# Second attention: both halves of a pair's values in one piece in the odd slot, a chunk in every even slot, and another order on ScalarE

## The chip, the cores and the metric

The kernel runs on one core of one Trainium2 chip. The metric is the device time of one launch in microseconds (us), the median of three runs. TensorE does the matmuls and transposes and writes PSUM; VectorE (DVE), ScalarE (ACT) and GpSimd (POOL) work beside it. Each engine runs its own list of instructions in order, and they meet at semaphores: `pe.wait_ge(ev("x"), k)` holds TensorE until counter x has reached k, and `.then_inc(ev("x"), 1)` raises it when the instruction ends.

## The reference, cut to what matters

Two blocks, each a layer norm with modulation, an attention and a feed-forward part. The change lies in the second block's attention, over x of shape 2 x 1024 x 128:

```python
H, Dk = 16, 64
q, k, v = shape(x @ Wq), shape(x @ Wk), shape(x @ Wv)      # b h s d
scores = einsum('bhqd,bhkd->bhqk', q, k)
weights = softmax(scores + position_bias, axis=-1)
context = einsum('bhqk,bhkd->bhqd', weights, v)
return context.transpose(0, 2, 1, 3).reshape(B, S, H * Dk) @ Wo
```

## The kernel before, in words

Two heads of one batch make a unit; there are 8 pairs of heads and 2 batches, so `UNITS = 16`. A unit has `TB = 8` tiles of 128 queries, `TILES = 128` in all. A tile n has two heads (hd 0 and 1) and goes through these steps:

- **Scores** (`pe_scores`, L407): 12 matmuls into `SC[0]` and `SC[1]`, one for each head. They wait for `nmax_done` of the tile before, since VectorE must have read `SC`.
- **Biased maximum** (`dve_biased`, L566): VectorE adds the position strip, writes `soft` and the maximum, once per head.
- **Exponential** (`act_exp`, L527): ScalarE, once per head, `ACTIVATE` and then `ACTIVATION_READ_ACCUMULATOR`, whose end is `exp_done`.
- **Turn** (`pe_turn`, L427): 16 transposes of one head into the two PT banks. Both heads use the same banks. So the second head's turn waits for `ptA_out`, ScalarE's copy of the first head's (`act_turned`, L512, 128x1024), and the next tile's first turn waits for the second head's two copies: VectorE's half (`dve_turned`, L574, `ptB_out`) and ScalarE's half (`act_turned_half`, L519, `ptB_half`).
- **Values** (`pe_values`, L444): two tiles (2g and 2g+1) make a group g, "pair" in the title; their turned weights lie in `PTs[:, g % 2]`. The values take 8 key blocks for 256 queries. They are done in two halves of 4 key blocks (16 matmul instructions each), half 0 in an even slot and half 1 in the next, odd one. ScalarE copies the result out (`act_ctx`, L536), at the end of the odd slot.
- **Output weights** (`pe_wo`, L463): in the next even slot, into the right half of `CX` and the left of `MI`, scaled by VectorE (`dve_wo`, L583) and added by POOL (`pool_add`, L607, L610).

Beside them go the **chunks**: the projections for the next unit, six for each, four of q and k (`pe_chunk`, L388) and two of v (L386), all in bank `MI`. ScalarE copies a chunk out (`act_chunk`, L330 or L321, `high_out`), POOL splits q and k into two parts (`pool_chunk`, L354 and L356, `low_out`). `pe_wo` writes `MI` too and so waits for the `high_out` of the chunk in its own slot.

The order is written out by hand in slots. Slot n holds, on TensorE: scores of tile n+1; turn of tile n, first head; a chunk if there is one; half the values of a group; turn of tile n, second head; in even slots the output weights. On ScalarE: the copy of the first turn; the exponential of tile n+1, first head; the chunk's copy; the exponential, second head; the half copy of the second turn; in odd slots `act_ctx`. From the third unit on the chunks lie in the slots `chunk_slots` of a unit, for the first two units in `second_slots` and `third_slots`, which fill every slot from 4 to 15. The last unit has no chunks after it.

Of the kernel before, what the change touches and what calls it, by code (L numbers as in the profile page):

```python
# [25 lines left out]
TB = S // P  # L26
# [18 lines left out]
TILES = UNITS * TB  # L45
GROUPS = TILES // 2
# [19 lines left out]
def build(nc, rel_hot, L0_attn_x, L0_attn_Wq, L0_attn_bq, L0_attn_Wk, L0_attn_bk, L0_attn_Wv, L0_attn_bv,  # L66
# [4 lines left out]
    with ExitStack() as ctx:  # L71
# [127 lines left out]
        def ev(name):  # L199

            if name not in sems:
                sems[name] = ctx.enter_context(nc.semaphore("s_" + name))
            return sems[name]
# [58 lines left out]

        chunks = [("q", 0), ("k", 0), ("q", 1), ("k", 1), ("v", 0), ("v", 1)]
        first_chunks = [("q", 0), ("k", 1), ("v", 1), ("k", 0), ("q", 1), ("v", 0)]
        chunk_slots = (0, 1, 2, 3, 5, 7)
        second_chunks = [("q", 0), ("k", 1), ("k", 0), ("q", 1), ("v", 0), ("v", 1)]
        second_slots, third_slots = (4, 5, 6, 7, 8, 9), (2, 3, 4, 5, 6, 7)

# [4 lines left out]
        def chunk_of(u, c):  # L273

            return (first_chunks, second_chunks, chunks)[min(u, 2)][c]
# [5 lines left out]
        def middle(n):  # L281

            u, i = n // TB, n % TB
            if n in chunk_at:
                return ("chunk",) + chunk_at[n]
            if u == UNITS - 1 and i in turn_slots:
                return "turn", turn_slots.index(i), 0
            return "none", 0, 0

        def chunks_until(n):  # L290

            return 6 + sum(1 for i in chunk_at if i <= n)

        def turns_until(n):

            return sum(1 for i in turn_slots if (UNITS - 1) * TB + i <= n)
# [13 lines left out]
        def chunk_bank(u, c):  # L310

            return four[c % 4] if u == 0 else MI[:, :]

        def act_chunk(act, u, c):

            kind, q = chunk_of(u, c)
            act.wait_ge(ev("proj_full"), 2 * (6 * u + c + 1))
            if kind == "v":
                if u >= 2:
                    act.wait_ge(ev("pv_done"), 4 * (u - 1))  # L320
                act.copy(V1[:, u % 2, 4 * q:4 * q + 4, :].rearrange("p t d -> p (t d)"), chunk_bank(u, c)).then_inc(ev("high_out"), 1)  # L321
                return
            sign = -1.0 if kind == "q" else 1.0
            if u == 0:
                act.mul(qk[0][:, 0 if kind == "q" else 2, q * CK:(q + 1) * CK], chunk_bank(u, c), sign).then_inc(ev("high_out"), 1)
                return

            if 4 * u + c >= 6:
                act.wait_ge(ev("low_out"), 4 * u + c - 1)
            act.mul(raw_qk[:, c % 2, :], chunk_bank(u, c), sign).then_inc(ev("high_out"), 1)  # L330
# [61 lines left out]
        def pe_scores(pe, n):  # L392

            u, i = n // TB, n % TB
            if n == 0:
                pe.wait_ge(ev("low_out"), 3)
            elif n == TB // 2 or i == 0 or (u == 1 and i == TB // 2):
                pe.wait_ge(ev("low_out"), 4 * u + (3 if (u, i) == (1, 0) else 4))
            if n == 0:
                pe.wait_ge(ev("hT_ready"), 10)  # L400
            else:
                pe.wait_ge(ev("nmax_done"), 2 * n)
            for k in range(2):
                for m, (qp, kp) in enumerate(((0, 2), (0, 3), (1, 2))):
                    for hd in range(2):
                        mine = slice(hd * DK, hd * DK + DK)
                        ins = pe.matmul(SC[hd][:, k * CK:(k + 1) * CK], qk[u % 2][mine, qp, i * P:(i + 1) * P],  # L407
                                        qk[u % 2][mine, kp, k * CK:(k + 1) * CK], start=(m == 0), stop=(m == 2))
                        if k == 1 and m == 2:
                            ins.then_inc(ev("scores"), 1)  # L410
# [21 lines left out]
        def pe_values(pe, g, half):  # L432

            if half == 0:
                pe.wait_ge(ev("ptA_out"), 2 * g + 2)
                pe.wait_ge(ev("ptB_out"), 2 * g + 2)
                pe.wait_ge(ev("ptB_half"), 2 * g + 2)
                pe.wait_ge(ev("ctx_out"), g)
            else:
                pe.wait_ge(ev("woA_out"), g)  # L440
            vb = g // 4 % 2
            for t in range(4 * half, 4 * half + 4):
                for hd in range(2):
                    ins = pe.matmul(CX[hd * DK:(hd + 1) * DK, 0:2 * P], V1[:, vb, t, hd * DK:(hd + 1) * DK],  # L444
                                    PTs[:, g % 2, hd, t, :], start=(t == 0), stop=(t == TB - 1))
                    if half == 1 and t == TB - 1:
                        ins.then_inc(ev("pv_done"), 1)

        def pe_wo(pe, g):

            u = g // 4
            n = 2 * g + 4
            pe.wait_ge(ev("ctx_out"), g + 1)
            if g >= 1:
                pe.wait_ge(ev("woB_out"), g)
            pe.wait_ge(ev("high_out"), chunks_until(n))
            if turns_until(n):
                pe.wait_ge(ev("wT_ready"), turns_until(n))
            for t in range(2):
                for hd in range(2):  # L460
                    mine = slice(hd * DK, hd * DK + DK)
                    dst = CX[:, (2 + t) * P:(3 + t) * P] if hd == 0 else MI[:, t * P:(t + 1) * P]
                    ins = pe.matmul(dst, ctxs[mine, g % 4, t * P:(t + 1) * P], wog[mine, u % B, u // B, :],  # L463
                                    start=(hd == 1 or (g == GROUPS - 1 and t == 0)), stop=True, skip_group_check=True)
                    if t == 1:
                        ins.then_inc(ev("woA_full" if hd == 0 else "woB_full"), 1)

        def pe_weights(pe, j):

            n = (UNITS - 1) * TB + turn_slots[j]  # L470
            if j == 0:
                pe.wait_ge(ev("ld_ffn"), 16 * 9)
                pe.wait_ge(ev("high_out"), 6 * UNITS)
            else:
                pe.wait_ge(ev("wT_ready"), j)
            pe.wait_ge(ev("woB_out"), (n - 5) // 2 + 1)
            for w in range(4 * j, min(4 * j + 4, 13)):
                ins = pe.transpose(MI[:, (w % 4) * P:(w % 4 + 1) * P], raw[:, w, :], ident[:, :])
            ins.then_inc(ev("ffn_turned"), 1)

        def pe_slot(pe, n):
            if n + 1 < TILES:
                pe_scores(pe, n + 1)
            if 0 <= n < TILES:
                pe_turn(pe, n, 0)
            what, a, c = middle(n)
            if what == "chunk":
                pe_chunk(pe, a, c)
            elif what == "turn":
                pe_weights(pe, a)  # L490
            if 2 <= n < TILES + 2:
                pe_values(pe, (n - 2) // 2, n % 2)
            if 0 <= n < TILES:
                pe_turn(pe, n, 1)
            if n >= 4 and n % 2 == 0:
                pe_wo(pe, (n - 4) // 2)

        def turned_in(hd):

            return PTW[:, :].rearrange("p (r t q) -> p r t q", r=2, t=TB)  # L500
# [6 lines left out]
        def act_turned(act, n):  # L507

            act.wait_ge(ev("ptA_full"), 2 * n + 2)
            if n >= 4:  # L510
                act.wait_ge(ev("pv_done"), n // 2 - 1)
            act.copy(turned_out(n, 0), turned_in(0)).then_inc(ev("ptA_out"), 1)  # L512

        def act_turned_half(act, n):

            act.wait_ge(ev("ptB_full"), 2 * n + 2)
            if n >= 4:
                act.wait_ge(ev("pv_done"), n // 2 - 1)
            act.copy(turned_out(n, 1)[:, 1, :, :], PT[1][:, :].rearrange("p (t q) -> p t q", t=TB)).then_inc(ev("ptB_half"), 1)  # L519
# [18 lines left out]
        def act_slot(act, n):  # L538
            if 0 <= n < TILES:
                act_turned(act, n)  # L540
            if n + 1 < TILES:
                act_exp(act, n + 1, 0)
            what, a, c = middle(n)
            if what == "chunk":
                act_chunk(act, a, c)
            elif what == "turn":
                act.wait_ge(ev("ffn_turned"), a + 1)
                w = min(4, 13 - 4 * a)
                act.copy(wT[:, 4 * a:4 * a + w, :].rearrange("p w d -> p (w d)"), MI[:, 0:w * P]).then_inc(ev("wT_ready"), 1)
            if n + 1 < TILES:  # L550
                act_exp(act, n + 1, 1)
            if 0 <= n < TILES:
                act_turned_half(act, n)
            if n >= 3 and n % 2 == 1:
                act_ctx(act, (n - 3) // 2)
# [1283 lines left out]
```

## Time and profile before

| | us |
|---|---|
| median of 3 runs (lowest to highest) | 948.13 (948.01 to 949.83) |
| the profiled execution, its own time | 956.01 |
| its span, first to last instruction | 954.3 |
| TensorE busy in the span | 902.3 (95%) |
| ScalarE busy | 642.4 (67%) |
| VectorE busy | 588.0 (62%) |
| GpSimd busy | 306.5 (32%) |

The trace is of one execution, whose own time is 0.8% over the median; rows are in its time. A busy share is an average over the span; TensorE's ends are modelled, so that its matmuls overlap in the rows. A start is given as us from the start of the span.

### The profile page before, as it was taken

To read this page: it belongs to the slowest core of one execution; us is meant where nothing else is said; L and a number is where in the kernel's file an instruction comes from. 1 tells how busy PE (TensorE), PEld (TensorE's weight loads), DVE (VectorE), ACT (ScalarE), POOL (GpSimd) and SP (SyncE) were. 2 spreads that over 40 slices of the span, in tenths; PEclk is the share of its full clock that TensorE was granted. 3 is DMA by queue.
4 is the path that set the end of the run, shared out by engine and by line. 5 is a ranking of instruction groups with operands and counts; after the bars stand their busy time and mean duration, and the time that the engine had idled before them with its cause. 6 is when DMAs were issued, how large, how long until landed. Compare 5 with 4: busy or idle time off the path is not lost. (4 is left out here: it accounts for less than half of the span.)

```text
span 954.3 us, 25417 instructions
## 1 busy us (share of the span) xinstructions
PE 902.3 (95%) x10209; PEld 665.0 (70%) x10209; DVE 588.0 (62%) x1348; ACT 642.4 (67%) x1094; POOL 306.5 (32%) x393
## 2 busy tenths in 40 slices
PE   8997994599999999999999999999999999998898
PEld 5685773376777776767777776767677776776677
DVE  6556112675666666666666666666666666676895
ACT  3551341487788777878787878887878778874244
POOL 5133803524423233241423333242322324115310
PEclk9998898799999999999999999999999999999899
DMA  8400621000020001002000200200020010000001
GB/s 240 155 2 23 213 88 53 26 1 2 2 92 2 3 25 70 2 2 93 1 3 1 93 2 2 92 2 2 2 92 2 2 33 10 3 1 2 1 12 34
DMA packets 27128, 35.48 MB, mean 37 GB/s; under 512 B 6042, under 2 KB 21716, under 8 KB 26836
## 3 DMA queue, kind: packets, MB, share of 16 engines
q1 hardware_dynamic: 25988, 31.76, 10.2%
q0 software_dynamic: 1024, 2.10, 0.7%
q8 instruction: 82, 1.34, 0.6%
q14 instruction: 34, 0.28, 0.1%
HBM read 28.48 MB, written 5.37 MB: 35 GB/s over the span
## 5 line engine op out<-in xcount | busy, mean ns | idle before, releaser
L566 DVE CUSTOM_DVE_ANT_0 soft<-SC,strips 128x1024 f32<-128x1024 f32 x256 | 303.3, 1222 | 78.3 <-PE SC L407 77.4
L527 ACT ACTIVATE soft<-soft,nmax 128x1024 f32<-128x1024 f32 x256 | 294.2, 1150 | 6.5 <-DVE nmax L566 6.5
L444 PE MATMUL CX<-PTs,V 128*64 128x256 f32 x2048 | 245.1, 381 | 0.0
L512 ACT COPY PTs<-PT 128x1024 f32<-128x1024 f32 x128 | 129.6, 1012 | 135.7 <-PE PT L427 135.7
L407 PE MATMUL SC<-qk 64*128 64x512 f32 x1536 | 210.8, 406 | 3.3 <-DVE nmax L566 1.8
L427 PEld LDWEIGHTS PT<-ident,soft 64*128 64x128 f32 x4096 | 159.6, 140 | 72.0 <-issue 32.5
L444 PEld LDWEIGHTS CX<-PTs,V 128*64 128x64 f32 x2048 | 143.0, 137 | 93.0 <-issue 35.5
L574 DVE COPY PTs<-PT 128x512 f32<-128x512 f32 x128 | 88.5, 692 | 164.5 <-PE PT L427 164.5
L427 PE MATMUL PT<-ident,soft 64*128 64x64 f32 x4096 | 177.1, 226 | 5.7 <-ACT soft L527 3.0
L407 PEld LDWEIGHTS SC<-qk 64*128 64x128 f32 x1536 | 136.7, 187 | 27.2 <-issue 2.1
L607 POOL TENSOR_TENSOR x<-x,wo_out 128x256 f32<-128x256 f32 x64 | 47.1, 736 | 209.3 <-DVE wo_out L583 209.3
L354 POOL CAST qk<-raw_qk 128x512 fp32r<-128x512 f32 x60 | 36.7, 612 | 237.0 <-ACT raw_qk L330 237.0
L356 POOL TENSOR_TENSOR qk<-raw_qk,qk 128x512 fp32r<-128x512 f32 x60 | 77.6, 1294 | 4.8
L519 ACT COPY PTs<-PT 128x512 f32<-128x512 f32 x128 | 74.0, 578 | 0.8 <-PE PT L427 0.7
L388 PE MATMUL MI<-hT,wpair 128*64 128x512 f32 x244 | 65.8, 617 | 0.9 <-ACT hT L863 0.9
L527 ACT ACTIVATION_READ_ACCUMULATOR soft<-soft,nmax 128x1 f32 x256 | 49.3, 193 | 0.0
L610 POOL TENSOR_TENSOR x<-x,wo_out 128x256 f32<-128x256 f32 x64 | 47.1, 735 | 5.0
L463 PE MATMUL CX<-wog,ctxs 64*128 64x128 f32 x256 | 42.4, 286 | 0.1
L463 PE MATMUL MI<-wog,ctxs 64*128 64x128 f32 x256 | 42.4, 286 | 0.0
L1005 ACT ACTIVATE probsT<-SC,cols 128x512 f32<-128x512 f32 x32 | 21.9, 689 | 26.7 <-PE SC L1757 26.6
L947 ACT ACTIVATE probsT<-SC,cols 128x384 f32<-128x384 f32 x32 | 18.6, 580 | 28.1 <-PE SC L1662 26.5
L330 ACT ACTIVATE raw_qk<-MI 128x512 f32<-128x512 f32 x60 | 35.2, 586 | 0.3 <-PE MI L388 0.3
(280 smaller groups left out, 999.8 us busy)
## 6 DMA issues: line engine op xcount, KB each, us to landing
strips<-bias_vec SPq DMA_DIRECT2D x8, 1920.0 KB, 8.3
arena<-in_L_ffn_w SPq DMA_DIRECT2D x1, 2048.0 KB, 12.4
slots_in<-arena SPq DMA_DIRECT2D x1, 1536.0 KB, 8.6
arena<-slots_in SPq DMA_DIRECT2D x8, 192.0 KB, 3.7
slots_out<-arena SPq DMA_DIRECT2D x8, 192.0 KB, 2.0
x<-in_L_attn_x SPq DMA_DIRECT2D x2, 512.0 KB, 4.3
out<-x SPq DMA_DIRECT2D x4, 256.0 KB, 2.3
arena<-in_L_wmod SPq DMA_DIRECT2D x2, 384.0 KB, 5.4
```

What stands on the lines that cost most here:

```text
L356: pool.tensor_tensor(qk[u % 2][:, k + 1, at], raw_qk[:, c % 2, :], qk[u % 2][:, k, at].bitcast(F32), ALU.subtract).then_inc(ev("low_out"), 1)
L388: ins = pe.matmul(bank[mine, :], wpair[:, p % 2, "qk".index(kind), mine], rhs, start=True, stop=True)
L407: ins = pe.matmul(SC[hd][:, k * CK:(k + 1) * CK], qk[u % 2][mine, qp, i * P:(i + 1) * P], qk[u % 2][mine, kp, k * CK:(k + 1) * CK], start= ...
L427: ins = pe.transpose(PT[r][:, t * DK:(t + 1) * DK], soft[mine, n % RING, hd, t * P:(t + 1) * P], ident[mine, mine])
L444: ins = pe.matmul(CX[hd * DK:(hd + 1) * DK, 0:2 * P], V1[:, vb, t, hd * DK:(hd + 1) * DK], PTs[:, g % 2, hd, t, :], start=(t == 0), stop=( ...
L463: ins = pe.matmul(dst, ctxs[mine, g % 4, t * P:(t + 1) * P], wog[mine, u % B, u // B, :], start=(hd == 1 or (g == GROUPS - 1 and t == 0)), ...
L512: act.copy(turned_out(n, 0), turned_in(0)).then_inc(ev("ptA_out"), 1)
L519: act.copy(turned_out(n, 1)[:, 1, :, :], PT[1][:, :].rearrange("p (t q) -> p t q", t=TB)).then_inc(ev("ptB_half"), 1)
L527: act.activation(soft[:, n % RING, hd, :], soft[:, n % RING, hd, :], ACT.Exp, bias=nmax[:, j:j + 1], scale=-1.0, accum_out=rsum[:, hd, n % ...
L566: dve.tensor_tensor_reduce(soft[:, n % RING, hd, :], SC[hd][:, :], strips[:, u // B % 2, hd, i * P:i * P + S], 1.0, 3.4e38, ALU.add, ALU.m ...
L574: dve.tensor_copy(turned_out(n, 1)[:, 0, :, :], PT[0][:, :].rearrange("p (t q) -> p t q", t=TB)).then_inc(ev("ptB_out"), 1)
L607: pool.tensor_tensor(x[:, t0:t0 + 2, :], x[:, t0:t0 + 2, :], wo_out[:, g % 2, 1, :, :], ALU.add).then_inc(ev("x_half"), 1)
```

## The change

The slots n from 6 to `TILES - TB - 1` = 119 are "joined". In them an even slot has no values, and the next odd slot has both halves, 32 matmul instructions in a row. The two v chunks of a unit move from slots 5 and 7 to the even slots 4 and 6. ScalarE's order in a joined even slot becomes: copy of the first turn; chunk; half copy of the second turn; exponential, first head; exponential, second head. Half 0 of the values gains a wait for `woA_out`, and the first output-weight matmul sets its start flag, since the joined values no longer stand between the two uses of `CX`.

```diff
-        chunk_slots = (0, 1, 2, 3, 5, 7)
+        chunk_slots = (0, 1, 2, 3, 4, 6)
...
+        def joined(n):
+            return 6 <= n < TILES - TB
...
                 pe.wait_ge(ev("ctx_out"), g)
-            else:
+            if half == 1 or joined(2 * g + 3):
                 pe.wait_ge(ev("woA_out"), g)
...
-                                    start=(hd == 1 or (g == GROUPS - 1 and t == 0)), stop=True, skip_group_check=True)
+                                    start=(hd == 1 or (t == 0 and (joined(n) or g == GROUPS - 1))), stop=True,
+                                    skip_group_check=True)
...
-            if 2 <= n < TILES + 2:
+            if joined(n) and n % 2 == 1:
+                pe_values(pe, (n - 3) // 2, 0)
+                pe_values(pe, (n - 3) // 2, 1)
+            elif 2 <= n < TILES + 2 and not joined(n):
                 pe_values(pe, (n - 2) // 2, n % 2)
...
                 act_turned(act, n)
+            what, a, c = middle(n)
+            early = joined(n) and n % 2 == 0
+            if early and what == "chunk":
+                act_chunk(act, a, c)
+            if early:
+                act_turned_half(act, n)
             if n + 1 < TILES:
                 act_exp(act, n + 1, 0)
-            what, a, c = middle(n)
-            if what == "chunk":
+            if what == "chunk" and not early:
                 act_chunk(act, a, c)
...
             if n + 1 < TILES:
                 act_exp(act, n + 1, 1)
-            if 0 <= n < TILES:
+            if 0 <= n < TILES and not early:
                 act_turned_half(act, n)
```

## Rows read from the trace of the kernel before

**Rows 1.** The page, busy time, share and instructions of each engine

```profile
PE 902.3 (95%) x10209; PEld 665.0 (70%) x10209; DVE 588.0 (62%) x1348; ACT 642.4 (67%) x1094; POOL 306.5 (32%) x393
```

**Rows 2.** Windows: stretch, its length, busy time of each engine, PEclk, DMA

```profile
415.40:458.04 42.64, 42.64 (x564) 30.83 (x564) 27.59 (x52) 34.07 (x59) 13.44 (x17) 1.00 0.14 53
500.67:841.74 341.07, 341.07 (x4488) 247.32 (x4488) 221.20 (x417) 272.73 (x465) 105.00 (x126) 1.00 0.07 24
```

**Rows 3.** Waits of all engines from 250 to 841 us, longest first

```profile
DVE PTs L574 <- PE PT L427: 141.3, 110, 1.6
ACT PTs L512 <- PE PT L427: 119.8, 111, 1.5
```

**Rows 4.** Timeline of TensorE, 500 to 522: start, length, operation [idle before]

```profile
500.52 1.64 PE L407 MATMUL SC<-qk 64*128 64x512 f32 x12
502.00 0.65 PE L427 MATMUL PT<-ident,soft 64*128 64x64 f32 x16
502.58 1.08 PE L388 MATMUL MI<-hT,wpair 128*64 128x512 f32 x4
503.49 1.90 PE L444 MATMUL CX<-PTs,V 128*64 128x256 f32 x16
505.32 0.71 PE L427 MATMUL PT<-ident,soft 64*128 64x64 f32 x16
505.86 0.33 PE L463 MATMUL CX<-wog,ctxs 64*128 64x128 f32 x1
...
506.28 1.63 PE L407 MATMUL SC<-qk 64*128 64x512 f32 x12
...
511.07 0.72 PE L427 MATMUL PT<-ident,soft 64*128 64x64 f32 x16
511.60 1.64 PE L407 MATMUL SC<-qk 64*128 64x512 f32 x12
...
513.66 1.95 PE L444 MATMUL CX<-PTs,V 128*64 128x256 f32 x16
515.54 0.71 PE L427 MATMUL PT<-ident,soft 64*128 64x64 f32 x16
```

**Rows 5.** Timeline of ScalarE and VectorE in the same even slot

```profile
502.72 1.01 ACT L512 COPY PTs<-PT 128x1024 f32<-128x1024 f32 x1 [0.80 <-PE PT L427]
...
504.49 0.08 DVE L566 DVE_READ_ACCUMULATOR2_ANT nmax<- 128x1 f32 x1
...
504.77 0.58 ACT L330 ACTIVATE raw_qk<-MI 128x512 f32<-128x512 f32 x1
505.25 1.15 ACT L527 ACTIVATE soft<-soft,nmax 128x1024 f32<-128x1024 f32 x1
...
506.29 0.19 ACT L527 ACTIVATION_READ_ACCUMULATOR soft<-soft,nmax 128x1 f32 x1
506.38 0.58 ACT L519 COPY PTs<-PT 128x512 f32<-128x512 f32 x1
```

**Rows 6.** Timeline, 188 to 197: TensorE released by ScalarE

```profile
188.40 0.19 ACT L527 ACTIVATION_READ_ACCUMULATOR soft<-soft,nmax 128x1 f32 x1
188.74 1.12 PE L427 MATMUL PT<-ident,soft 64*128 64x64 f32 x16 [3.00 <-ACT soft L527]
195.59 1.01 ACT L512 COPY PTs<-PT 128x1024 f32<-128x1024 f32 x1 [1.65 <-PE PT L427]
196.74 0.71 PE L427 MATMUL PT<-ident,soft 64*128 64x64 f32 x16 [1.21 <-ACT PTs L512]
```

**Rows 7.** Timeline of slot 4, 211 to 214: a chunk directly ahead of a turn

```profile
211.97 1.06 PE L388 MATMUL MI<-hT,wpair 128*64 128x512 f32 x4
212.96 0.72 PE L427 MATMUL PT<-ident,soft 64*128 64x64 f32 x16
213.07 0.60 ACT L330 ACTIVATE raw_qk<-MI 128x512 f32<-128x512 f32 x1 [0.27 <-PE MI L388]
```

**Rows 8.** Timeline, 225 to 227: the end of slot 6

```profile
225.20 1.26 POOL L356 TENSOR_TENSOR qk<-raw_qk,qk 128x512 fp32r<-128x512 f32 x1
226.52 1.68 PE L407 MATMUL SC<-qk 64*128 64x512 f32 x12 [0.90 <-POOL qk L356]
```

**Rows 9.** Windows after a gap on TensorE, columns as in Rows 2

```profile
188.00:191.00 3.00, 1.12 (x16) 0.96 (x16) 1.36 (x4) 2.83 (x6) 2.92 (x3) 0.56 0.03 8
226.00:232.00 6.00, 5.48 (x66) 3.70 (x68) 2.92 (x6) 3.29 (x6) 2.44 (x4) 1.00 0.00 0
```

## The prediction

> **What bounds the kernel now.** I read the page first: TensorE is busy for 95% of the span, ScalarE for 67%, VectorE for 62% [rows 1]. Since its ends are modelled, "busy" alone proves little, so the windows come next: in a whole unit of eight slots (415.40 to 458.04) and in the eight units from 500.67 on, TensorE is busy for every microsecond of the window, at a granted clock of 1.00, its level of 2.4 GHz [rows 2]. The waits from 250 to 841 us name no semaphore wait of the matmul stream; ScalarE and VectorE wait for TensorE instead, 119.8 us ahead of the copy of the first turn and 141.3 ahead of the half copy of the second [rows 3]. The timeline then shows how: in an even slot the first turn starts at 502.00, the chunk at 502.58, the values at 503.49, the second turn at 505.32, the output weights at 505.86, the next scores at 506.28, each where the stream of the one before runs out [rows 4]. So TensorE's stream sets the pace of this stage: an even slot with chunk takes 506.28 - 500.52 = 5.76 us, the odd one 511.60 - 506.28 = 5.32, the pair 11.08. Anything that makes TensorE wait here is paid in full; nothing that frees another engine is worth anything.
>
> The reader should also see what keeps TensorE from waiting. Between the two turns lies ScalarE's copy, which occupies 502.72 to 503.73 [rows 5]; TensorE works on chunk and values from 502.58 to 505.32 meanwhile, so this copy has 1.6 us to spare. Without a chunk the values alone (513.66 to 515.54, 1.88 us [rows 4]) still cover it.
>
> **What the change takes from TensorE's stream.** Nothing is removed: the same matmuls, turns and chunks, the same count. A slot has a middle part of the form 128\*64 (chunk, values) between turns and scores of the form 64\*128. Before, eight slots have eight such parts. After, an even slot's is its chunk alone and an odd slot's is the chunk, if any, and 32 value matmuls: eight again, because every even slot gets a chunk. What changes is the length of a part. Sixteen value matmuls take 1.83 us from their start to the turn behind a chunk (503.49 to 505.32) and 1.88 where they follow a turn [rows 4]. They go in pairs, and eight pairs of 256 columns at the rate at which four chunk instructions of 512 columns take 0.91 (502.58 to 503.49, two pairs, so 0.23 per 256 columns at most) are 1.7 to 1.8; I take 1.71 for a second half that has neither way in nor way out, a saving of 0.12. Against it a chunk that is followed by a turn costs 0.99 (211.97 to 212.96 [rows 7]) where it costs 0.91 ahead of values: 0.08 back. Net -0.04 us a pair, with 0 and -0.12 as its bounds.
>
> The Trainium skill, TensorEngine Tiling (Array Packing), section Key Properties, says that changing the tiling mode drains TensorE, which is the rule that would speak for the joined piece. It would be worth something only if a change of mode vanished; by the count above none does, and the rows give the chunk alone its own way out. Had the even slot lost its part, the sum below would be better by 0.12 to 0.17 a pair, 7 to 10 us in all. It has not.
>
> **What the change takes from TensorE's cover.** In an even slot only the chunk is left between the two turns. Take E as the end of the first turn's matmuls (502.65, that is 2.13 after the scores' start [rows 4]).
>
> First stall. The copy starts 0.07 after E and lasts 1.01 [rows 5], so it ends at 1.08. TensorE starts a turn 0.14 after such a copy (195.59 + 1.01 = 196.60, turn at 196.74 [rows 6]): second turn at E + 1.22. Freely it would start at -0.07 + 0.99 = E + 0.92. So 0.30 us of waiting. The scores follow 0.96 after the second turn's start (505.32 to 506.28 [rows 4]), at E + 2.18. An even slot is then 2.13 + 2.18 = 4.31 us.
>
> Two other waits in it are nearly as late, and are hidden. The output weights wait for the chunk's copy: that one can start when its matmuls are out, 0.04 after their end (213.03 to 213.07 [rows 7]), about E + 1.06, and ends 0.58 later [rows 5], so that TensorE has it at 1.79 against 1.76 needed. The next scores wait for VectorE's maximum, whose last row ends at 504.57 [rows 5], 4.05 after the slot's start, 4.2 with a hand-over like the others; that is ahead of 4.31 by 0.1.
>
> Second stall. ScalarE's new order puts the chunk's copy and the half copy ahead of both exponentials. The second turn's matmuls end at 1.22 + 0.71 = 1.93 [rows 6]; the half copy starts some 0.05 later and takes 0.58 [rows 5], to 2.56. The exponential follows 0.10 before that end, as the one at 505.25 does behind the copy that ends at 505.35, and from its start to the end of its accumulator read (506.29 + 0.19) it takes 1.23 [rows 5]: 3.69. The tile's first turn comes 0.15 later (188.40 + 0.19 = 188.59 to 188.74 [rows 6]), at E + 3.84. Freely it would start 1.48 after the scores (500.52 to 502.00 [rows 4]), at 2.18 + 1.48 = 3.66. So 0.18 of waiting, and a turn that starts late takes 0.71 where one whose weights came in behind the scores takes 0.65 [rows 4, 6]: 0.06 more. Before, that exponential stood directly behind the first turn's copy, ahead of the chunk's. Half copy and exponential are queued behind a wait for `ptB_full`, and this is what TensorE is made to wait for.
>
> The odd slot behind it has 3.54 us of values (1.83 + 1.71) as cover; there every copy and both exponentials of the next tile end before the second turn. VectorE's half copy and `dve_wo` come sooner, with room. POOL sees each chunk sooner; the new wait of half 0 for `woA_out` is for a result some 2 us old by then; DMA isn't touched. These edits cost nothing while the values cover them; if they did not, they would be part of the third rival.
>
> **Sum.** Pair before: 11.08. Pair after: even 4.31; odd 2.13 + 0.18 + 0.06 to the end of its first turn, then -0.07 + 0.91 + 3.54 + 0.52 (511.07 to 511.60 [rows 4]) = 4.90, together 7.27. So 11.58, or +0.50: two stalls of 0.30 and 0.24, less 0.04. A v chunk behaves alike, and a pair with one chunk instead of two has the same cover in its even slot. Joined are the slots 6 to 119, 57 pairs: 57 x 0.50 = 28.5 us. Slot 6 is special: the scores behind it wait for POOL's split of its chunk, 0.90 us before the change [rows 8]. In the new order that split starts about 1.1 us sooner, but the scores want it 1.83 sooner, so this wait grows by about 0.7 and hides the second stall: 0.4 more than another pair. Total +29 us. Against the profiled execution this is 956.01 + 29 = 985; against the median of the runs, 0.8% lower by its own start and end, 948.1 + 29 = 977.
>
> **The rivals.**
> 1. *Only the first stall* (the exponential is in time, by shorter hand-overs or because scores behind a late turn run longer): 57 x 0.26 = 15, so 963. For it: the second stall is a difference of 0.18 between sums of four rows. Against: all four are rows of this trace.
> 2. *Both stalls hidden, no change*: TensorE's stream is the same, so 948. It needs the copy and its two hand-overs, 1.22, to fit under 0.92. The copy alone is 1.01 in the rows. Little speaks for it.
> 3. *A third wait is added*: VectorE's maximum is only 0.1 ahead of the scores, and the chunk's copy is level with the output weights. If each is later by 0.2, the pair pays 0.1 to 0.2 more, as `dve_wo` and the half copy now fall into a slot of 4.3 us: 57 x 0.2 = 11 on top, 989, up to 995.
> 4. *Faster*: the joined values save their way in and out, 0.12 a pair, and the chunk covers the copy after all. The place is the even slot's second turn; the price is 57 x -0.12 = -7, so 941; it decides only from a second turn at E + 0.92 or sooner, with the exponential at 3.36 or sooner. The rows speak against both.
> A lower clock I leave out: behind 3.00 us of idleness the granted clock was 0.56, a mix of the 1.2 and 2.4 GHz levels, but behind the gap of 0.90 at slot 6 it stayed at 1.00 [rows 6, 8, 9], and the new gaps are a third of that.
>
> **How the numbers follow.** A measurement of this kernel tells about 0.2% (2 us) from no change. Forecast (0.40 to 0.65 a pair, 971 to 985): 0.66. Rival 1 (960 to 971): 0.13. Rival 3 (985 to 995): 0.14. Rival 2: 0.03. Rival 4: 0.04. The range reaches into rivals 1 and 3: 0.28 a pair (964) to 0.74 (990). Slower 0.93, same 0.03, faster 0.04.
>
> **What would show it.** In the profile after, TensorE's waits should have two new lines: the turn waiting for ScalarE's copy (L512), 57 times, near 0.3 us each, and the turn waiting for the exponential (L527), near 0.2 to 0.3. An even slot should be 4.3 us, an odd one with chunk 7.3, without one 6.4, a unit of eight slots 44.6 instead of 42.64. Value matmuls should show no idleness between the halves. I am wrong if TensorE is still gapless, if the even slot is near 4.0 (no first stall), or if its scores wait for VectorE.

## The result: 976.0 us, 2.8% slower, and the profile after

| | before | after |
|---|---|---|
| median, us | 948.07 | 976.0 (974.68 to 976.93, 4 runs) |
| ratio | | 1.0282, 95% interval 1.0257 to 1.0307 |
| span of the profiled execution | 954.3 | 972.9 |

The forecast was 977.0, with a range from 964 to 990. The page, busy time of each engine (answers to [rows 1]):

```profile
PE 913.4 (94%) x10209; PEld 674.9 (69%) x10209; DVE 590.9 (61%) x1348; ACT 655.5 (67%) x1094; POOL 306.1 (31%) x393
```

The windows of the changed kernel: first one unit of eight slots (answers to the first of [rows 2]), then the stretch from the scores of tile 7 to those of tile 121, which holds all 57 joined pairs:

```profile
371.98:416.32 44.34, 43.51 (x568) 31.68 (x564) 27.82 (x52) 34.96 (x58) 13.41 (x17) 1.00 0.01 2
212.91:848.51 635.60, 622.46 (x8016) 452.64 (x8012) 396.42 (x741) 499.99 (x831) 194.61 (x232) 1.00 0.07 24
```

The same stretch of the kernel before:

```profile
219.60:830.51 610.91, 610.01 (x8015) 441.04 (x8012) 393.23 (x741) 486.49 (x830) 194.67 (x232) 1.00 0.07 25
```

A unit takes 44.34 us where it took 42.64, the stage 635.60 where it took 610.91: 24.7 us more, 0.43 for each of the 57 pairs. The granted clock is 1.00 in both. The medians differ by 27.9, with an interval of about 24 to 29. Below, "the stage" is always this stretch. Ahead of it, in code that no kernel here changes, the profiled executions take between 212.5 and 219.6 us, so the stage separates causes more sharply than the medians do. Inside it pairs of the same form repeat to about 0.01 us: the two-chunk pairs of the kernel before have a mean of 11.08, and those of kernels 8 and 9 below, whose edits don't touch them, have the same to 0.01. From the third unit on, a pair with one chunk is 0.41 to 0.42 longer than before and one with two chunks 0.44.

Waits from 250 to 841 us of the changed kernel (answers to [rows 3]): who waits for whom, us in total, times, longest.

```profile
ACT PTs L527 <- PE PT L431: 67.4, 106, 1.2
...
ACT PTs L520 <- PE PT L431: 58.2, 54, 1.1
PEld PT L431 <- issue: 39.6, 53, 1.1
PEld PT L431 <- ACT soft L535: 33.8, 106, 0.4
...
PE PT L431 <- ACT PTs L520: 11.1, 53, 0.2
```

The last line is new. TensorE's turn (L431) waits for ScalarE's copy (L520) once in every pair. The 0.2 us in it is counted from the modelled end of the chunk's matmuls; the weight load ahead of it (PEld) is idle for up to 1.1. The other line that was forecast, the turn waiting for the exponential, isn't there for the matmuls. It is there for their weight loads: 33.8 us, 106 times, where the kernel before has 21.5, 56 times. The timeline of TensorE shows one pair, an even and an odd slot, as [rows 4] do for before:

```profile
505.23 1.64 PE L411 MATMUL SC<-qk 64*128 64x512 f32 x12
...
506.70 0.66 PE L431 MATMUL PT<-ident,soft 64*128 64x64 f32 x16
507.29 1.08 PE L392 MATMUL MI<-hT,wpair 128*64 128x512 f32 x4
508.59 0.72 PE L431 MATMUL PT<-ident,soft 64*128 64x64 f32 x16 [0.22 <-ACT PTs L520]
509.18 0.34 PE L467 MATMUL CX<-wog,ctxs 64*128 64x128 f32 x1
...
509.62 0.47 PE L411 MATMUL SC<-qk 64*128 64x512 f32 x1
...
511.12 0.71 PE L431 MATMUL PT<-ident,soft 64*128 64x64 f32 x16
511.76 1.08 PE L392 MATMUL MI<-hT,wpair 128*64 128x512 f32 x4
512.67 3.62 PE L448 MATMUL CX<-PTs,V 128*64 128x256 f32 x32
516.23 0.71 PE L431 MATMUL PT<-ident,soft 64*128 64x64 f32 x16
516.75 1.63 PE L411 MATMUL SC<-qk 64*128 64x512 f32 x12
```

ScalarE in the same even slot (answers to [rows 5]):

```profile
507.43 1.01 ACT L520 COPY PTs<-PT 128x1024 f32<-128x1024 f32 x1 [1.08 <-PE PT L431]
508.44 0.60 ACT L334 ACTIVATE raw_qk<-MI 128x512 f32<-128x512 f32 x1
509.34 0.59 ACT L527 COPY PTs<-PT 128x512 f32<-128x512 f32 x1 [0.30 <-PE PT L431]
509.82 1.16 ACT L535 ACTIVATE soft<-soft,nmax 128x1024 f32<-128x1024 f32 x1
510.88 0.19 ACT L535 ACTIVATION_READ_ACCUMULATOR soft<-soft,nmax 128x1 f32 x1
```

Read them together, start to start. The copy ends at 508.44 and the second turn starts at 508.59, 1.30 after the chunk where the stream alone gives 0.99 [rows 7]: 0.31 lost. The chunk's copy ends at 509.04 and the output weights' first matmul starts at 509.18; from the second turn to the scores it is 1.03 where it was 0.96: 0.07. The accumulator read ends at 511.07 and the next first turn starts at 511.12, 1.50 after the scores where the odd slots before have 1.47; and the turn is followed by the chunk after 0.64 where it was 0.59: 0.08 together. Its weight load starts with it at 511.12, while before, in the same place (507.75), it started 0.23 ahead. The values go on for 3.56 us (512.67 to 516.23), 1.83 + 1.73, without a gap between the halves; before, the two halves took 1.83 and 1.82. The pair is 11.52 where it was 11.08: 0.31 + 0.07 + 0.08 lost, 0.08 more for a chunk directly ahead of a turn [rows 7], 0.10 less for the values and the odd slot's end, 0.44 in all. How the 0.39 between chunk and second turn (1.30 for 0.91) divides into 0.31 of waiting and 0.08 of stream rests on the one row of [rows 7].

### The profile page after: what moved, and what is told of

The parts are those of the page before. It is cut to its first block and busy times, and to the rows that moved or that the text cites. A ratio compares the mean times of both kernels' runs of the same rounds, so it can differ in the third digit from the quotient of the medians.

```text
span 972.9 us, 25417 instructions
## 1 busy us (share of the span) xinstructions
PE 913.4 (94%) x10209; PEld 674.9 (69%) x10209; DVE 590.9 (61%) x1348; ACT 655.5 (67%) x1094; POOL 306.1 (31%) x393
## 5 line engine op out<-in xcount | busy, mean ns | idle before, releaser
L448 PE MATMUL CX<-PTs,V 128*64 128x256 f32 x2048 | 237.8, 384 | 0.0
L431 PEld LDWEIGHTS PT<-ident,soft 64*128 64x128 f32 x4096 | 155.5, 139 | 96.3 <-issue 49.4
L448 PEld LDWEIGHTS CX<-PTs,V 128*64 128x64 f32 x2048 | 145.0, 138 | 85.5 <-issue 20.5
L431 PE MATMUL PT<-ident,soft 64*128 64x64 f32 x4096 | 179.2, 227 | 14.6 <-ACT PTs L520 14.3
L520 ACT COPY PTs<-PT 128x1024 f32<-128x1024 f32 x128 | 128.7, 1006 | 73.3 <-PE PT L431 73.3
L411 PEld LDWEIGHTS SC<-qk 64*128 64x128 f32 x1536 | 144.3, 186 | 21.0 <-issue 1.7
L623 POOL TENSOR_TENSOR x<-x,wo_out 128x256 f32<-128x256 f32 x64 | 47.2, 737 | 5.0
L467 PE MATMUL MI<-wog,ctxs 64*128 64x128 f32 x256 | 45.9, 300 | 0.0
L1018 ACT ACTIVATE probsT<-SC,cols 128x512 f32<-128x512 f32 x32 | 21.9, 690 | 24.8 <-PE SC L1770 24.7
```

The source lines that it names most:

```text
L431: ins = pe.transpose(PT[r][:, t * DK:(t + 1) * DK], soft[mine, n % RING, hd, t * P:(t + 1) * P], ident[mine, mine])
```

## The experiments

All ratios are against the kernel before on the same chip, with a 95% interval; "stage" is the distance in TensorE's timeline from the scores of tile 7 to those of tile 121.

| kernel | median, us | ratio | stage, us | against before |
|---|---|---|---|---|
| the change | 976.0 | 1.0282 (1.0257 to 1.0307) | 635.60 | +24.7 |
| 1. v chunks moved, no more | 955.59 | 1.0062 (1.0040 to 1.0084) | 616.29 | +5.4 |
| 2. that and ScalarE's new order | 973.25 | 1.0239 (1.0199 to 1.0279) | 631.10 | +20.2 |
| 3. joined, old order | 1029.62 | 1.0832 (1.0786 to 1.0878) | 690.98 | +80.1 |
| 4. the change, exponential between | 973.54 | 1.0245 (1.0204 to 1.0286) | 633.50 | +22.6 |
| 5. one key block in the even slot | 960.63 | 1.0126 (1.0095 to 1.0157) | 621.49 | +10.6 |
| 6. that, exponential between | 951.49 | 1.0015 (0.9996 to 1.0034) | 611.62 | +0.7 |
| 7. the change, v chunks back | 997.74 | 1.0515 (1.0482 to 1.0548) | 658.15 | +47.2 |
| 8. before, chunk first in slot 6 | 948.61 | 0.9990 (0.9974 to 1.0007) | 610.06 | -0.85 |
| 9. kernel 1, half copy first | 950.1 | 0.9992 (0.9967 to 1.0018) | 611.06 | +0.15 |
| 10. kernel 2, half copy first | 960.04 | 1.0087 (1.0058 to 1.0116) | 620.97 | +10.1 |

**1. The chunks' places alone.**

```diff
-        chunk_slots = (0, 1, 2, 3, 5, 7)
+        chunk_slots = (0, 1, 2, 3, 4, 6)
```

> The kernel before with one edit: the v chunks in slots 4 and 6 instead of 5 and 7. My theory (TensorE's stream is unchanged and values still cover every copy): no change, 948 us, ratio 0.999 to 1.001, and TensorE without idleness in the stage. Rival (a chunk in the even slot, ahead of the output weights that share its bank, costs by itself): each of 26 pairs pays about 0.1 us, 951 us.

It is slower by 0.6%, which neither theory had. The timeline of a chunkless odd slot and the start of the next slot shows a wait that I hadn't looked for:

```profile
398.91 0.19 ACT L527 ACTIVATION_READ_ACCUMULATOR soft<-soft,nmax 128x1 f32 x1
399.00 1.14 ACT L527 ACTIVATE soft<-soft,nmax 128x1024 f32<-128x1024 f32 x1
...
399.21 1.64 PE L407 MATMUL SC<-qk 64*128 64x512 f32 x12
399.47 0.69 DVE L574 COPY PTs<-PT 128x512 f32<-128x512 f32 x1 [0.67 <-PE PT L427]
...
400.13 0.57 ACT L519 COPY PTs<-PT 128x512 f32<-128x512 f32 x1
...
400.85 0.71 PE L427 MATMUL PT<-ident,soft 64*128 64x64 f32 x16
```

An odd slot with half the values and no chunk is only 4.45 us long. ScalarE's copy and two exponentials stand ahead of its half copy, which ends at 400.70; the next first turn, which needs the banks, starts at 400.85, 1.64 after the scores instead of 1.47, and is followed by the chunk 0.06 late as well. VectorE's half, in the same banks, had been done at 400.16. There are 26 such odd slots, and the stage ends before the turn behind the last of them, so it holds 25 of these waits. The even slots behind them are 0.216 longer than in kernel 9, where the wait is gone: 25 x 0.216 = 5.4, as measured. The window of this stage shows no idleness for it:

```profile
213.59:829.88 616.29, 615.38 (x8016) 439.69 (x8012) 393.28 (x741) 486.41 (x830) 195.16 (x232) 1.00 0.07 25
```

TensorE is idle for 0.91 us there, as before for 0.90: that is the wait at the end of slot 6 [rows 8]. The 5.4 us more are in none of its idle time: TensorE's ends are modelled, and these 25 stalls of 0.2 us disappear under them. Only the distance from start to start shows them.

**9. The same with the half copy moved.** The order of ScalarE in the chunkless odd slots from 7 to 119:

```diff
+            soon = n % 2 == 1 and 6 <= n < TILES - TB and what == "none"
+            if soon:
+                act_turned_half(act, n)
             if n + 1 < TILES:
                 act_exp(act, n + 1, 1)
-            if 0 <= n < TILES:
+            if 0 <= n < TILES and not soon:
                 act_turned_half(act, n)
```

> The run with the v chunks in slots 4 and 6 alone (stage 616.29 us from the scores of tile 7 to those of tile 121, against 610.91 before), plus one edit: in the odd slots 7 to 119 that have no chunk, ScalarE makes the half copy of the second turn ahead of the second head's exponential. Theory: with half the values and no chunk such a slot is 4.45 us, ScalarE's copy and two exponentials stand ahead of the half copy, and the next first turn waits for it 0.23 us in 26 slots; with the half copy first that wait is gone: stage 610.9 to 611.3, time as before, 948. Rival (the wait is for something else, such as VectorE's half or the tile's exponential): the stage stays at 616.

The timeline of such a slot's end in this kernel:

```profile
401.09 1.64 PE L407 MATMUL SC<-qk 64*128 64x512 f32 x12
401.35 0.59 ACT L519 COPY PTs<-PT 128x512 f32<-128x512 f32 x1 [0.37 <-PE PT L427]
401.35 0.69 DVE L577 COPY PTs<-PT 128x512 f32<-128x512 f32 x1 [0.67 <-PE PT L427]
401.83 1.15 ACT L527 ACTIVATE soft<-soft,nmax 128x1024 f32<-128x1024 f32 x1
...
402.56 0.66 PE L427 MATMUL PT<-ident,soft 64*128 64x64 f32 x16
```

The turn follows the scores by 1.47 again and the stage is back at 611.06. So the place of the v chunks costs 5.4 us by this one wait, and by nothing else.

**2. ScalarE's new order without the joining.** Kernel 1 with the change's `act_slot`; the values stay half and half.

> The kernel before with the v chunks in slots 4 and 6 and with ScalarE's new order in the even slots 6 to 118; the values stay split half and half. Theory: no first stall, since values cover the copy; the exponential comes 2.53 us after the second turn's start, as in the changed kernel's trace, where the stream would want it after 2.44, and a turn that starts late takes 0.06 more: 0.15 a pair, 57 x 0.15 = 8.5, so 956 to 957 us. Rival 1 (the new order is the whole cost, the joining is free): 976. Rival 2 (the second stall exists only because the cover is gone): 948.

The first part came as expected: in odd slots the first turn starts 1.59 after the scores and its chunk follows after 0.64, 0.18 a pair. But there is a second wait, behind chunkless odd slots:

```profile
401.81 1.64 PE L411 MATMUL SC<-qk 64*128 64x512 f32 x12
...
402.92 0.57 ACT L523 COPY PTs<-PT 128x512 f32<-128x512 f32 x1
...
403.63 0.72 PE L431 MATMUL PT<-ident,soft 64*128 64x64 f32 x16 [0.18 <-ACT PTs L523]
```

The new order pushes the even slot's exponentials into the odd one, so ScalarE is later still with the half copy there: the turn comes 1.82 after the scores instead of 1.47, and its chunk 0.07 late, 0.42 against the kernel before. With 25 of these in the stage (10.5) and 56 x 0.18 = 10.1 this makes 20.6, less 1.0 for the pair of slots 6 and 7, which is shorter than before: 19.6 of the 20.2 measured. The median is 16 us above what was expected (956 to 957) and only 3 below the first rival's 976, but kernel 10 shows that half of the stage's loss is this second wait, which neither had. The profiled execution took 967.97 us, the shortest of five; the median of 973.25 is further from before than the stage's 20.2.

**10. The same with the half copy moved,** as in kernel 9.

> The run with ScalarE's new order but values split half and half (stage 631.11 us), plus the same edit in the odd slots without a chunk. Theory: its stalls are two, 57 of 0.18 us where an odd slot's first turn waits for the exponential, and 26 of 0.42 where an even slot's waits for the late half copy; the edit removes the second kind, 10.9 us: stage about 620 to 621, time 957 to 959. Rival (the odd slot is late as a whole since the exponentials of the even slot were pushed into it, and moving one copy only moves the wait): stage above 626.

```profile
215.67:836.64 620.97, 620.97 (x8015) 435.51 (x8012) 393.17 (x741) 493.51 (x829) 195.51 (x232) 1.00 0.07 24
```

Stage 620.97: 10.1 less than kernel 2, where 10.9 was expected for 26 waits; it holds 25, and the even slots concerned are 0.405 shorter: 25 x 0.405 = 10.1. The two causes are separate and add up. What is left is one stall of 0.18 in each of 56 pairs, 10.1 us against before, in a window in which TensorE is busy for 620.97 of 620.97 us.

**3. Joined, with ScalarE's old order.**

```diff
             if 0 <= n < TILES:
                 act_turned(act, n)
-            what, a, c = middle(n)
-            early = joined(n) and n % 2 == 0
-            if early and what == "chunk":
-                act_chunk(act, a, c)
-            if early:
-                act_turned_half(act, n)
             if n + 1 < TILES:
                 act_exp(act, n + 1, 0)
...
```

> The changed kernel with ScalarE's old order in every slot. Theory: the joining itself is what costs and the new order softens it. With the old order the chunk's copy ends 2.70 us after the first turn's end, the output weights wait for it, the scores come at 3.25 and the next first turn at 4.73 where the changed kernel has 3.76: 57 x 0.97 = 55 more, about 1031 us, with the output weights waiting some 1 us for the chunk's copy 57 times. Rival (the new order is what costs, undoing it mends the change): 948 to 960.

Its stage is 55.4 longer than the change's; forecast were 55. Waits from 250 to 850 us:

```profile
PE CX L467 <- ACT raw_qk L334: 22.8, 25, 0.9
PE CX L467 <- ACT V L325: 22.5, 25, 0.9
```

Fifty times in this window TensorE waits 0.9 us ahead of the output weights, for the chunk's copy. An even slot is 5.42 us instead of 4.40, an odd one 0.05 shorter. The new order thus keeps the joined kernel's loss from being three times as large; what it costs there by itself is kernel 4's question.

**4. The first exponential ahead of the half copy.**

```diff
-            if early:
-                act_turned_half(act, n)
             if n + 1 < TILES:
                 act_exp(act, n + 1, 0)
+            if early:
+                act_turned_half(act, n)
```

> The changed kernel with the first head's exponential between the chunk's copy and the half copy in the even slots. Theory: the first stall stays (second turn 1.30 us after the chunk's start), the exponential is no longer what the next first turn waits for, and that turn follows the scores by the stream's 1.48 and takes 0.65: 0.08 a pair less, 971 to 972 us. Rival (the second stall is as large as I forecast, 0.24): 962. Rival (something else than the exponential holds that turn): 976.

The time is 2.5 lower than the change's by the medians, which their intervals don't separate; the stage is 2.1 shorter, 0.04 a pair, half of the 0.08 expected. The exponential is not what the turn waits for any more: it comes 1.47 after the scores (510.64 to 512.11). But the scores themselves still come 1.04 after the second turn instead of 0.96, since the output weights still wait for the chunk's copy, and the turn takes 0.62 to the chunk instead of 0.58; why it isn't 0.58 is open. From the second turn to the next first one it is 2.51 here, 2.53 in the change and 2.44 in the stream.

**5 and 6. One key block of values stays in the even slot.** The values are split 1 to 7, on top of kernel 1, with the change's order (5) and with that of kernel 4 (6).

```diff
-            for t in range(4 * half, 4 * half + 4):
+            cut = 1 if joined(2 * g + 3) else 4
+            for t in range(cut) if half == 0 else range(cut, TB):
```

> Values split 1 to 7 instead of 0 to 8 (the change) or 4 to 4 (before): one key block, 4 matmul instructions, some 0.43 us, stays in the even slot behind the chunk, the other seven go to the odd slot; v chunks in slots 4 and 6, ScalarE's new order in even slots. Theory: 0.43 covers the first stall of 0.31, so the second turn starts as the stream allows, and the second stall of about 0.15 a pair stays: 956 to 957 us, the same as with the order alone. Rival (what costs is the length of the values piece in the odd slot, not the cover in the even one): 970 or more.

> As the run with one key block in the even slot, but with the first head's exponential between the chunk's copy and the half copy. Theory: both stalls are gone, TensorE is without a gap again: 948 us, ratio 0.999 to 1.002. Rival (moving values to the odd slot has a cost of its own that isn't a stall, such as the rate of the value matmuls): 951 or more.

TensorE's timeline in an even slot of kernel 6:

```profile
411.56 1.08 PE L392 MATMUL MI<-hT,wpair 128*64 128x512 f32 x4
412.47 0.60 PE L449 MATMUL CX<-PTs,V 128*64 128x256 f32 x4
413.01 0.71 PE L431 MATMUL PT<-ident,soft 64*128 64x64 f32 x16
413.56 0.33 PE L468 MATMUL CX<-wog,ctxs 64*128 64x128 f32 x1
```

Four value instructions (0.54 to the turn) are enough cover: the second turn comes at 1.45 after the chunk's start, where the copy would let it go at 1.30. With the change's order 10.6 us are left (56 x 0.18 = 10.1, and 0.24 for slots 6 and 7), with the other order 0.7. So seven eighths of the values can sit in the odd slot for nothing. The last eighth costs 21.9 us by kernels 4 and 6, which have the same order on ScalarE, and 14.1 by the change and kernel 5. And the order is worth 9.9 with one key block in the even slot (5 against 6) and 2.1 with none (the change against 4): its stall and the wait of the output weights overlap. The median of kernel 6, 951.49, is level with the rival's "951 or more", but that of the kernel before was 950.03 in the same set of executions; the two are not told apart.

**7. The change with the v chunks back in slots 5 and 7,** `chunk_slots = (0, 1, 2, 3, 5, 7)`; 26 even slots have nothing between their turns.

> The changed kernel with the v chunks back in the odd slots 5 and 7, so that 26 even slots have nothing between their two turns. Theory: such a slot is as long as before, since the chain of copies sets its length, and the chunk's 0.92 us is added to the odd slot in full, less the 0.05 that its output weights no longer wait: 26 x 0.87 = 23 more than the changed kernel, about 998 us. Rival (a change of mode that vanishes is worth 0.12 to 0.17): 3 to 4 less, 994. Rival (the even slot gets shorter without its chunk): 976 to 985.

TensorE in such an even slot:

```profile
355.38 1.64 PE L411 MATMUL SC<-qk 64*128 64x512 f32 x12
356.85 0.67 PE L431 MATMUL PT<-ident,soft 64*128 64x64 f32 x16
358.73 0.72 PE L431 MATMUL PT<-ident,soft 64*128 64x64 f32 x16 [1.21 <-ACT PTs L520]
...
359.67 0.47 PE L411 MATMUL SC<-qk 64*128 64x512 f32 x1
```

The turns are 1.88 us apart with nothing between them, against 1.89 with a chunk between (506.70 to 508.59 above). The scores do come sooner behind the second turn, 0.94 instead of 1.03, as the output weights have no chunk's copy to wait for. But the next first turn starts at 361.27, 2.54 after the second turn where the change has 2.53: it waits for the exponential's accumulator read (ends at 361.21) all the same. So the chunk in the even slot is free, and the wait of the output weights costs nothing while the exponential is later. The stage is 22.6 longer than the change's, as the sum of 26 x 0.87 had it, though not for its reason: the 0.05 that the chunk costs less than 0.92 is not the output weights' wait but the values, which take 3.55 behind a chunk and 3.61 behind a turn. What a vanished change of mode is worth can't be read here, since it would lie inside the wait.

**8. Before, with slot 6's chunk copied first.**

```diff
+            what, a, c = middle(n)
+            if n == 6:
+                act_chunk(act, a, c)
             if n + 1 < TILES:
                 act_exp(act, n + 1, 0)
...
-            if what == "chunk":
+            if what == "chunk" and n != 6:
```

> The kernel before with one edit: in slot 6 alone ScalarE copies the chunk ahead of the first head's exponential. Theory: TensorE's wait of 0.90 us for POOL's split at the end of slot 6 goes away, since the split starts 1.1 us sooner: 947.2 us, ratio 0.999. It would be the only gap of the stage left to close. Rival (another wait takes its place there): 948.

The pair of slots 6 and 7 takes 11.26 us instead of 12.28 and the stage is 0.85 shorter. The ratio's interval holds 1, so of the time itself nothing is shown. The other pairs are unchanged. It is the only one of these kernels with a stage shorter than before's.

## Why the prediction was right

- *TensorE's stream sets the pace, and a wait is paid in full.* Right. Kernels 3 and 7 moved the stage by 55.4 and 22.6 against the change, where sums of start-to-start distances had 55 and 23; kernels 5, 6 and 9 by 10.6, 0.7 and 0.15 against before, where they had 8.5, 0 and 0 to 0.4. Kernels 1 and 2, whose sums had 0 and 8.5, moved it by 5.4 and 20.2: the rule held, but a wait was missing from the list. But the evidence that I gave for a gapless stream, windows without idleness, would have shown the same with the stalls of kernel 1. The distances in [rows 4] carried the claim, not the windows.
- *The stream itself hardly changes.* Right: the second half adds 1.73 (1.71 forecast); the 0.99 of the chunk alone can't be read in the change, where it lies inside the wait; kernel 6, with nearly all values moved, leaves the stage as it was.
- *First stall, 0.30.* Right: 0.31, the turn 1.23 after the end of the first turn's matmuls where 1.22 was forecast. Kernels 5 and 6 show its cause by covering it.
- *Second stall, 0.24.* The mechanism was right and the size too large: 0.15. From the second turn to the next first one it is 2.53 where 2.62 was forecast and the stream has 2.44, and the late turn takes 0.06 more. I took the hand-over from the accumulator read to TensorE as 0.15, from a row behind 3.00 us of idleness; here it is 0.05 (511.07 to 511.12), and in kernel 2 too.
- *The output weights' wait for the chunk's copy is hidden.* Right in what it costs, though it can be seen: it holds the scores for 0.07, and those 0.07 are a part of the 0.15, not on top of it. Kernel 7's slots without the wait reach the next first turn no sooner (2.54). It shows by itself only where the exponential is out of the way, in kernel 4.
- *Sum.* 0.44 for an ordinary pair in the timeline against 0.50; the pair of slots 6 and 7 0.69 longer (12.97 against 12.28) where 0.9 was forecast; the stage +24.7 against +29. The medians' difference is 27.9. That 977 came within 1 us of 976.0 is luck: the terms were 4 us too large, and 3 us came from outside the stage, where executions differ by more than that. Later sets of executions had the kernel before at 948.4, 950.03 and 951.66, against which 976.0 would be 24 to 28 more. No cause in the change was looked for or found there.
- *What I did not see:* in parts, the change is not additive. Moving the v chunks costs 5.4 us alone, by a late half copy at the end of a short odd slot, and the new order raises that to 10. In the change this wait is gone, because the odd slot has 3.6 us of values. The prediction found room for every copy in the odd slot, which was right for the whole change and wrong for its parts. Joining on top of kernel 2 adds only 4.5 us.
- *Rivals.* Rival 1 (only the first stall, 963) falls: the rest of the pair's loss is 0.15, not zero, and kernel 5, whose first stall is covered, still loses 10.6. Rival 3's wait for VectorE does not appear: its last maximum ends at 509.28, and the scores start at 509.62. Rivals 2 and 4 needed a second turn 0.31 earlier.

## What to carry to other kernels

When one engine's stream is the bound, list for each of its waits the chain that must finish in time and the work that covers it, and check the shortest slot that the new order makes: here 1.2 us of copy and hand-over needed 1.2 us of matmuls, 0.9 were left, and one key block more, 0.45 us, was enough (kernels 5 and 6). In this kernel moving work to another slot cost nothing where it was moved to; it cost where it was taken from, the values from the even slot in the change and the chunk from the odd slot in kernel 1. Read stalls from the distance between starts, since a stretch without idle time can hold a 0.2 us stall in every pair of slots, as in kernel 10.

## What was not expected of the hardware

A turn of TensorE started 0.15 us after ScalarE's copy had ended (508.44 to 508.59; the same for the half copy of kernel 1, 400.70 to 400.85), but 0.05 after the end of an accumulator read (511.07 to 511.12). A turn whose weight load began only with it took 0.06 us longer to the next matmul, beside the wait itself (0.64 against 0.58, where the load began 0.23 ahead).
